# Attention and mixture of experts on one core: the inputs laid out on the host as the kernel holds them

## The chip, the core and the metric

The kernel runs on one core of a Trainium2 chip. A core has five engines that work side by side and meet at semaphores: TensorE (PE, matrix products, with weight loads PEld), VectorE (DVE), ScalarE (ACT), GpSimd (POOL) and SyncE (SP), which here only issues DMAs. SBUF is the memory that all of them work in, PSUM the one into which PE writes. The metric is the device time of one execution in microseconds.

## What is computed

Eight sequences of 256 rows of 256 numbers attend to a context of 120 rows each, and the result goes through a layer of eight experts. Biases are not zero.

```python
x = x + xattn(layernorm(x), ctx, mask)      # 16 heads of 64, keys and values from ctx (120 rows)
#   q = LN(x) @ Wq + bq ; k = ctx @ Wk + bk ; v = ctx @ Wv + bv
#   softmax(where(mask, -inf, q k^T / 8)) v, then @ Wo + bo
z = layernorm(x)
#   probs = softmax(z @ Wg), the two largest of 8, their weights normalized
#   out = sum over chosen e of w_e * (silu(z @ W1[e] + b1[e]) @ W2[e] + b2[e])
#   shared = silu(z @ Ws1 + bs1) @ Ws2 + bs2
x = x + out + 0.1 * shared
```

## The kernel before

All tensors are float32. A product is made of three on PE: each operand is split into a high part (ScalarE writes it, rounded to the PE's format, as `..._hi`) and a low part (the rest, a subtraction on VectorE or GpSimd, `..._lo`), and `three` (L301 to L305) issues high by high, high by low and low by high.

The rows are worked on in four groups of two sequences, four tiles of 128 rows each. For each group the attention runs over 8 pairs of heads (`PAIRS`); the loop variable n counts the 32 pairs of all groups, g = n // 8 and p = n % 8. In an iteration PE makes the scores of pair n, turns the probabilities of pair n - 1 (`transposes`), makes queries and keys of a later pair (`qk`), and the attention product of pair n - 1 (`attend`). VectorE takes the maxima of the scores (L673), copies the turned probabilities from PSUM (pT, L684), ScalarE takes exponentials (L1106) and writes the queries (qh, L1085), GpSimd multiplies the probabilities by their reciprocal sums (pr, L488). Each engine's order is the order of the code; there is no planner.

Before a group's queries can be made, its rows and its context must stand turned and split. In iteration p = 6 PE turns the next group's rows (`turn_rows`, L1275, into two PSUM banks) and its context (`turn_context`, L1285, four turns into bank_m). ScalarE writes the high parts xT_hi (L1070) and cT_hi (L1074), VectorE the low parts xT_lo (L648) and cT_lo (L653), in `x_turned` and then `c_turned`. ctxb holds the context as it lies in memory, 120 rows on 120 partitions.

For the first group all this stands at the start. Statistics of the rows (VectorE, L613 and L623) go to GpSimd's rsqrt (rstd, L460), VectorE normalizes (xrows, L630), PE turns. While nothing is there for PE it turns the identity (`warm`, L1290). The biases bq, bk, bv, bs1 and b1 come by five DMAs into 96 rows (brows), are turned by PE (L1433) and copied by ScalarE to bias_t (L1131), where a bias stands as a column. VectorE scales the query bias in bias_t (L734) before ScalarE may write qh. Weights come in nine pieces (`PIECES`, `load_piece`) of raw values; `piece_hi` on ScalarE (L1065) and `piece_lo` on VectorE (L636, pieces 0, 1, 4, 5) or GpSimd (L481, the others) split them:

```python
for name, h, part in (("k", 0, 2), ("q", 0, 2), ("v", 0, 1), ("v", 1, 1), ("q", 1, 2), ("k", 1, 2), ("q", 1, 1), ("k", 1, 1)):
```

A piece of part 2 is a quarter of the columns (two pairs), of part 1 a half. `next_group` on SyncE loads mask, rows and context of a later group when the tiles are free. In the attention stage GpSimd also splits the experts' second weights in pieces of 512 columns (praw, L495 and L497), which SyncE loads and stores back. After attention and the shared layer come the experts: their first weights (`load_w1`, `load_w1n`) are 1024 KB each.

## Time and profile before

| | us |
|---|---|
| median of three runs | 623.38 |
| lowest, highest | 623.11, 623.4 |
| the profiled execution | 623.21 |
| its span, first to last instruction | 621.5 |
| PE busy in it | 603.9 |
| DVE, ACT, POOL busy | 363.1, 371.6, 311.6 |

The profile is of one execution. An engine's busy time is the sum of its instructions; PE is the one that is nearly always busy. A row of the timeline shows when an instruction (or several like it in a row, as x4) starts and how long it lasts; in brackets behind it stands how long its engine had been idle and which engine's work released it. An instruction's recorded start can lie before it gets what it needs inside the engine, so a long duration of a small instruction is a wait as well.

### The profile page before, as it was taken

Reading aid. Unit: us, or ns where it says so; the run is one execution under the profiler, and the core shown is the slowest. Engines: PE = TensorE matmul, PEld = TensorE weight load, DVE = VectorE, ACT = ScalarE, POOL = GpSimd, SP = SyncE. Lnnn points to the kernel's source line nnn. Section 1 sums busy time; section 2 is a strip of 40 time slices with the busy share of each in tenths; the row PEclk is TensorE's granted clock in tenths of the full one; section 3 lists DMA queues with packets and bytes.
Section 4 is the critical chain, followed back from the end, with each engine's and each line's share of the span. In section 5 each row is a group of like instructions: output and inputs, shape, how many; then the busy total and the mean of one; then the engine's idle time right before and its main releaser. Section 6 shows DMA issues by size and latency. Waiting matters only on the chain.

```text
span 621.5 us, 13278 instructions
## 1 busy us (share of the span) xinstructions
PE 603.9 (97%) x4711; PEld 536.1 (86%) x4711; DVE 363.1 (58%) x740; ACT 371.6 (60%) x1036; POOL 311.6 (50%) x307
## 2 busy tenths in 40 slices
PE   7999999999999999999999999999999999999996
PEld 5876797779776887678988999999999999999996
DVE  5576617772577437675798444756564646564632
ACT  4778608771578428756354465948484848484742
POOL 4977527874479629745170531126443553443343
PEclk9999999999999999999999999999999999999999
DMA  9401452256234553300224449996979897989341
GB/s 291 142 2 52 137 168 90 104 164 194 92 131 138 154 187 118 100 22 0 90 86 170 139 136 279 308 377 195 327 222 332 221 360 206 335 214 324 84 138 18
DMA packets 57582, 106.35 MB, mean 171 GB/s; under 512 B 8173, under 2 KB 30734, under 8 KB 55598
## 3 DMA queue, kind: packets, MB, share of 16 engines
q1 hardware_dynamic: 42094, 63.44, 31.6%
q10 hardware_dynamic: 7840, 32.30, 14.1%
q0 software_dynamic: 7584, 9.76, 7.8%
q8 instruction: 39, 0.64, 0.4%
q14 instruction: 25, 0.20, 0.1%
HBM read 80.24 MB, written 26.16 MB: 171 GB/s over the span
## 4 chain that ended last, share of the span: by engine, by line
PE 73%; ACT 9%; DVE 8%; POOL 4%; issue 4%; DMA 1%; POOLq 0%; ACTq 0%; DVEq 0%
ACT pr L1106 7%; PE bank_s L303 4%; PE bank_t L305 4%; PE bank_t L304 4%; PE bank_t L303 4%; PE bank_s L304 4%; PE bank_s L305 4%; PE bank_s L1600 4%; PE bank_m L303 4%; PE bank_q L303 4%; PE bank_q L305 4%; PE bank_m L304 4%; PE bank_q L304 4%; PE bank_m L305 4%; PE bank_k L304 3%
## 5 line engine op out<-in xcount | busy, mean ns | idle before, releaser
L597 POOL DMA_INDIRECT out_dram<-yw,xs x39 | 65.2, 1671 | 124.2 <-DMA out_dram<-yw,xs 74.9
L1106 ACT ACTIVATE pr<-bank_s,nmax 128x120 f32<-128x120 f32 x256 | 88.2, 371 | 42.6 <-DVE nmax L673 42.3
L1007 DVE TENSOR_TENSOR hh_lo<-hbT,hh_hi 128x512 fp32r<-128x512 f32 x78 | 53.9, 692 | 68.6 <-ACT hh_hi L1236 65.8
L488 POOL TENSOR_TENSOR pr<-pr,rsum 128x480 f32<-128x480 f32 x64 | 62.7, 987 | 61.1 <-DVE rsum L677 60.7
L1233 ACT ACTIVATE hbT<-bank_s,b_col 128x256 f32<-128x256 f32 (+1 forms) x120 | 42.5, 420 | 68.2 <-PE bank_s L305 26.4
L575 POOL DMA_INDIRECT xs<-rows_d,sorted_i x39 | 44.5, 1141 | 61.9 <-issue 29.7
L1106 ACT ACTIVATION_READ_ACCUMULATOR pr<-bank_s,nmax 128x1 f32 x256 | 55.5, 217 | 0.0
L1236 ACT ACTIVATE hh_hi<-hbT 128x512 fp32r<-128x512 f32 x78 | 49.3, 632 | 2.5
L1085 ACT ACTIVATE qh<-bank_q,bias_t 128x512 f32<-128x512 f32 x32 | 22.6, 706 | 44.1 <-PE bank_q L305 41.5
L673 DVE TENSOR_REDUCE nmax<-bank_s 128x4 f32<-128x480 f32 x64 | 38.9, 650 | 6.4 <-PE bank_s L1359 5.8
L497 POOL TENSOR_TENSOR zg_lo<-praw,zg_hi 128x512 fp32r<-128x512 f32 x32 | 41.1, 1283 | 2.6
L1359 PEld LDWEIGHTS bank_s<-kh,qh 64*128 64x128 f32 x512 | 31.1, 187 | 13.0 <-issue 8.4
L1194 ACT ACTIVATE xg<-bank_s,bias_t 128x512 f32<-128x512 f32 x32 | 22.0, 688 | 32.9 <-PE bank_s L305 30.5
L684 DVE COPY pT<-bank_t 120x512 f32<-120x512 f32 x64 | 41.0, 682 | 1.0 <-PE bank_t L1371 1.0
L1359 PE MATMUL bank_s<-kh,qh 64*128 64x120 f32 x512 | 37.0, 284 | 1.8 <-ACT qh L1085 1.8
L1387 PE MATMUL bank_o<-pT,vals 120*64 120x256 f32 x256 | 34.7, 392 | 3.4 <-DVE pT L684 3.1
L1371 PE MATMUL bank_t<-ident,pr 128*120 128x128 f32 x256 | 35.9, 280 | 1.5 <-POOL pr L488 1.3
L689 DVE SCALAR_TENSOR_TENSOR aT_lo<-bank_o,bias_t,aT_hi 128x512 fp32r<-128x512 f32 x32 | 23.9, 747 | 15.9 <-ACT aT_hi L1112 15.9
L1371 PEld LDWEIGHTS bank_t<-ident,pr 128*120 128x120 f32 x256 | 27.1, 138 | 6.5 <-POOL pr L488 3.3
L1387 PEld LDWEIGHTS bank_o<-pT,vals 120*64 120x64 f32 x256 | 15.5, 136 | 14.8 <-DVE pT L684 7.0
L303 PE MATMUL bank_q<-xT_hi,wq_hi 128*128 128x512 f32 x64 | 27.6, 432 | 0.1
L495 POOL CAST zg_hi<-praw 128x512 fp32r<-128x512 f32 x32 | 19.6, 611 | 16.2 <-DMA praw<-in_L_ffn_W 16.1
(368 smaller groups left out, 2126.8 us busy)
## 6 DMA issues: line engine op xcount, KB each, us to landing
praw<-in_L_ffn_W SPq DMA_DIRECT2D x32, 256.0 KB, 2.8
w2s<-zg_hi SPq DMA_DIRECT2D x32, 256.0 KB, 3.5
w2s<-zg_lo SPq DMA_DIRECT2D x32, 256.0 KB, 3.6
aT_hi<-w2s SPq DMA_DIRECT2D x32, 256.0 KB
aT_lo<-w2s SPq DMA_DIRECT2D x32, 256.0 KB
w2n_hi<-w2s ACTq DMA_DIRECT2D x6, 1024.0 KB
w2n_lo<-w2s ACTq DMA_DIRECT2D x6, 1024.0 KB
wq_raw<-in_L_ffn_W ACTq DMA_DIRECT2D x5, 1024.0 KB
```

What stands on the lines that cost most here:

```text
L303: nc.tensor.matmul(o, st(0), mo(0), start=first, stop=False)
L304: nc.tensor.matmul(o, st(0), mo(1), start=False, stop=False)
L305: return nc.tensor.matmul(o, st(1), mo(0), start=False, stop=last)
L488: nc.gpsimd.tensor_tensor(pt, pt, rsum[:, n % 2, h, :].rearrange("p (t a) -> p t a", a=1).broadcast_to([P, GT, SK]), ALU.mult).then_inc(s[ ...
L575: nc.gpsimd.indirect_dma_start(out=xs[:, q % XU, :], out_offset=None, in_=rows_d, in_offset=bass.IndirectOffsetOnAxis(ap=sorted_i[:, ROWS[ ...
L597: nc.gpsimd.indirect_dma_start(out=out_f, out_offset=bass.IndirectOffsetOnAxis(ap=xs[:, q % XU, C:C + 1].bitcast(U32), axis=0), in_=yw[:, ...
L1007: nc.vector.tensor_tensor(hh_lo[:, n % 2, u, :], hbT[:, i % 4, :], hh_hi[:, n % 2, u, :].bitcast(F32), ALU.subtract).then_inc(s["hh_lo_s"], 1)
L1106: last = nc.scalar.activation(pr[:, n % 2, h, t, :], bank_s[h][:, t * SK:(t + 1) * SK], ACT.Exp, bias=nmax[st], accum_out=ssum[st])
L1236: nc.scalar.activation(hh_hi[:, n % 2, u, :], hbT[:, i % 4, :], ACT.Copy).then_inc(s["hh_hi_s"], 1)
L1359: last = nc.tensor.matmul(bank_s[h][:, t * SK:(t + 1) * SK], qh[r, n % 2, t * P:(t + 1) * P], kh[r, n % 2, b * SK:(b + 1) * SK], start=Fal ...
L1371: last = nc.tensor.transpose(bank_t[h][0:SK, t * P:(t + 1) * P], pr[:, n % 2, h, t, :], ident[:, :])
L1387: last = nc.tensor.matmul(bank_o[h * D:(h + 1) * D, b * S:(b + 1) * S], vals[:, b, c:c + D], pT[:, h, b * QT:(b + 1) * QT, :], start=True, ...
```

## The change

The host hands every input over in the order in which the kernel holds it; the bytes that are loaded stay the same. Rows and masks come by groups with the partition first, weights by pairs (Wq, Wk) or halves (Wv) of columns, the experts' weights with the partition ahead of the 128-row blocks, all biases as one array of 128 x 96, and the context already turned, 128 x 2 x 240. The arrays in SBUF keep their sizes, save that ctxb is now 128 partitions and brows is gone; wq, wk and wv stand in their tiles by pairs or halves, and PE's operands are read from there.

With that go: PE's four turns of the context per group, its turn of the biases, ScalarE's copy of them, and the wait of the scores for it. At the start PE turns the identity 26 times in one piece. cT_hi and cT_lo are made from ctxb and no longer from PSUM, and they come ahead of xT_hi and xT_lo for the later groups; for the first group VectorE makes cT_lo ahead of the normalized rows.

```diff
-        ctxb = sb("ctxb", [SK, GB, C], F32, a)
+        ctxb = sb("ctxb", [P, KC, GB * SK], F32, a)
...
-        for name, h, part in (("k", 0, 2), ("q", 0, 2), ("v", 0, 1), ("v", 1, 1), ("q", 1, 2), ("k", 1, 2), ("q", 1, 1), ("k", 1, 1)):
+        for name, first, size in (("k", 0, 2), ("q", 0, 2), ("v", 0, 1), ("v", 1, 1), ("q", 2, 2), ("k", 2, 2), ("q", 4, 4), ("k", 4, 4)):
...
-            eng.dma_start(w1_raw[w % W1_HOMES], w1[bass.ds(e, 1), :, :].rearrange("a (k p) n -> p (a k) n", p=P)).then_inc(w1_in[w % W1_HOMES], 16)
+            eng.dma_start(w1_raw[w % W1_HOMES], w1[bass.ds(e, 1), :, :, :].rearrange("a p k n -> p (a k) n")).then_inc(w1_in[w % W1_HOMES], 16)
...
-                    sp.wait_ge(s["ct"], g)
-                    sp.dma_start(ctxb[:, :, :], ctx_v[:, g * GB:(g + 1) * GB, :]).then_inc(s["ctx_in"], 16)
+                    sp.wait_ge(s["ct_lo"], g)
+                    sp.dma_start(ctxb[:, :, :], ctx_in[g]).then_inc(s["ctx_in"], 16)
...
                 def c_turned(g):
                     dve.wait_ge(s["ct_hi"], g + 1)
-                    nc.vector.tensor_tensor(cT_lo[:, :, :].rearrange("p k n -> p (k n)"), bank_m[:, 0:KC * GB * SK],
-                                            cT_hi[:, :, :].bitcast(F32).rearrange("p k n -> p (k n)"),
-                                            ALU.subtract).then_inc(s["ct_lo"], 1)
+                    nc.vector.tensor_tensor(cT_lo[:, :, :], ctxb[:, :, :], cT_hi[:, :, :].bitcast(F32), ALU.subtract).then_inc(s["ct_lo"], 1)
...
+                c_turned(0)
                 normalize(x_tile, "ln1", 0, lambda t: xrows[:, t, 0:C])
-                c_turned(0)
                 piece_lo(0)
...
                     if g + 1 < G and p == PAIRS - 2:
+                        c_turned(g + 1)
                         x_turned(g + 1)
-                        c_turned(g + 1)
...
-                row = 0
-                for v in (bq, bk, bv, bs1):
-                    r = v.rearrange("(a p) -> a p", p=P)
-                    act.dma_start(brows[row:row + r.shape[0], :], r).then_inc(s["brow_in"], 16)
-                    row += r.shape[0]
-                act.dma_start(brows[row:, :], b1.rearrange("e (f p) -> (e f) p", p=P)).then_inc(s["brow_in"], 16)
-                act.dma_start(wg_raw[:, :, :], wg.rearrange("(k p) n -> p k n", p=P)).then_inc(s["wg_in"], 16)
+                act.dma_start(bias_t[:, :], biases).then_inc(s["biased"], 16)
+                act.dma_start(wg_raw[:, :, :], wg).then_inc(s["wg_in"], 16)
...
                 def c_turned(g):
-                    act.wait_ge(s["ct"], g + 1)
-                    nc.scalar.activation(cT_hi[:, :, :], bank_m[:, 0:KC * GB * SK], ACT.Copy).then_inc(s["ct_hi"], 1)
+                    act.wait_ge(s["ctx_in"], 16 * (g + 1))
+                    if g:
+
+                        act.wait_ge(s["qk_k"], g * PAIRS)
+                        act.wait_ge(s["vp"], 4 * g)
+                    nc.scalar.activation(cT_hi[:, :, :], ctxb[:, :, :], ACT.Copy).then_inc(s["ct_hi"], 1)
...
-                act.wait_ge(s["b_t"], 1)
-                nc.scalar.activation(bias_t[:, :], bank_s[1][:, 0:NBIAS], ACT.Copy).then_inc(s["biased"], 1)
...
+                    if g >= 2 and h == 0:
+                        pe.wait_ge(s["lgc"], g - 1)
...
-                warm(16)
-                turn_context(0)
-                warm(8)
+                warm(26)
                 turn_rows(0)
-                pe.wait_ge(s["brow_in"], 80)
-                nc.tensor.transpose(bank_s[1][:, 0:NBIAS], brows[:, :], ident[0:NBIAS, 0:NBIAS]).then_inc(s["b_t"], 1)
-                warm(4)
                 key(0)
...
                     elif p == PAIRS - 2 and more:
                         turn_rows(g + 1)
-                        turn_context(g + 1)
```

VectorE at the start, before. xg are the raw rows, mv mean and variance, wk_lo and wq_lo the low parts of the first weight pieces:

```order
L623 BN_AGGR mv<-stats 128x2 x4
L630 TENSOR_SCALAR xrows<-xg,mv,rstd 128x256 x4
L653 TENSOR_TENSOR cT_lo<-bank_m,cT_hi 128x480
L636 TENSOR_TENSOR wk_lo<-wk_raw,wk_hi 128x2x256
L636 TENSOR_TENSOR wq_lo<-wq_raw,wq_hi 128x2x256
L648 TENSOR_TENSOR xT_lo<-bank_q,xT_hi 128x512
L648 TENSOR_TENSOR xT_lo<-bank_o,xT_hi 128x512
L642 TENSOR_SCALAR maskb<-masku 128x480
L734 TENSOR_SCALAR bias_t<-bias_t 128x8
```

The same place after:

```order
L617 BN_AGGR mv<-stats 128x2 x4
L647 TENSOR_TENSOR cT_lo<-ctxb,cT_hi 128x480
L624 TENSOR_SCALAR xrows<-xg,mv,rstd 128x256 x4
L630 TENSOR_TENSOR wk_lo<-wk_raw,wk_hi 128x512
L630 TENSOR_TENSOR wq_lo<-wq_raw,wq_hi 128x512
L642 TENSOR_TENSOR xT_lo<-bank_q,xT_hi 128x512
L642 TENSOR_TENSOR xT_lo<-bank_o,xT_hi 128x512
L636 TENSOR_SCALAR maskb<-masku 128x480
L726 TENSOR_SCALAR bias_t<-bias_t 128x8
```

cT_lo moved from behind the normalization to ahead of it.

ScalarE at the start, before:

```order
L1074 ACTIVATE cT_hi<-bank_m 128x480
L1065 ACTIVATE wk_hi<-wk_raw 128x2x256
L1065 ACTIVATE wq_hi<-wq_raw 128x2x256
L1070 ACTIVATE xT_hi<-bank_q 128x512
L1070 ACTIVATE xT_hi<-bank_o 128x512
L1131 ACTIVATE bias_t<-bank_s 128x96
L1065 ACTIVATE wv_hi<-wv_raw 128x2x512
L1085 ACTIVATE qh<-bank_q,bias_t 128x512
```

and after:

```order
L1065 ACTIVATE cT_hi<-ctxb 128x480
L1052 ACTIVATE wk_hi<-wk_raw 128x512
L1052 ACTIVATE wq_hi<-wq_raw 128x512
L1057 ACTIVATE xT_hi<-bank_q 128x512
L1057 ACTIVATE xT_hi<-bank_o 128x512
L1052 ACTIVATE wv_hi<-wv_raw 128x1024
L1076 ACTIVATE qh<-bank_q,bias_t 128x512
```

The copy of the biases between xT_hi and wv_hi is gone.

VectorE in front of the second group (iteration p = 6 and on), before:

```order
L677 RECIPROCAL rsum<-ssum 128x4 x2
L648 TENSOR_TENSOR xT_lo<-bank_q,xT_hi 128x512
L648 TENSOR_TENSOR xT_lo<-bank_k,xT_hi 128x512
L653 TENSOR_TENSOR cT_lo<-bank_m,cT_hi 128x480
L689 SCALAR_TENSOR_TENSOR aT_lo<-bank_o,bias_t,aT_hi 128x512
L673 TENSOR_REDUCE nmax<-bank_s 128x4 x2
```

and after:

```order
L669 RECIPROCAL rsum<-ssum 128x4 x2
L647 TENSOR_TENSOR cT_lo<-ctxb,cT_hi 128x480
L642 TENSOR_TENSOR xT_lo<-bank_q,xT_hi 128x512
L642 TENSOR_TENSOR xT_lo<-bank_k,xT_hi 128x512
L681 SCALAR_TENSOR_TENSOR aT_lo<-bank_o,bias_t,aT_hi 128x512
L665 TENSOR_REDUCE nmax<-bank_s 128x4 x2
```

cT_lo stands first of the three splits, and its first input is ctxb in SBUF.

## Rows read from the trace of the kernel before

**Rows 1.** The page: engine table (busy us, share, instructions) and DMA packets.

```profile
PE 603.9 (97%) x4711; PEld 536.1 (86%) x4711; DVE 363.1 (58%) x740; ACT 371.6 (60%) x1036; POOL 311.6 (50%) x307
...
DMA packets 57582, 106.35 MB, mean 171 GB/s; under 512 B 8173, under 2 KB 30734, under 8 KB 55598
```

**Rows 2.** Busy time by stage: from:to, length, busy (instructions), clock share, DMA, GB/s.

```profile
0.00:15.10 15.10, 10.45 (x58) 8.75 (x58) 9.09 (x21) 5.80 (x10) 6.77 (x18) 1.00 0.91 288
30.00:80.00 50.00, 49.25 (x383) 37.30 (x382) 32.41 (x77) 36.80 (x148) 34.03 (x36) 1.00 0.20 66
400.00:450.00 50.00, 49.79 (x426) 49.62 (x425) 28.27 (x51) 30.16 (x64) 23.78 (x16) 1.00 0.92 302
```

The engines stand in the order PE, PEld, DVE, ACT, POOL.

**Rows 3.** Timeline of the start: start us, us, engine, line, operation [idle <-releaser].

```profile
5.95 1.06 PE L1285 MATMUL bank_m<-ident,ctxb 120*128 120x120 f32 x4 [0.19 <-DMA ctxb<-in_ctx]
...
6.31 1.05 POOL L460 TENSOR_TENSOR rstd<-vareps,mhalf 128x4 f32<-128x4 f32 x1
...
7.40 1.38 DVE L630 TENSOR_SCALAR xrows<-xg,mv,rstd 128x256 f32<-128x256 f32 x4 [1.45 <-POOL rstd L460]
...
8.70 0.65 DVE L653 TENSOR_TENSOR cT_lo<-bank_m,cT_hi 128x480 fp32r<-128x480 f32 x1
...
9.53 0.60 ACT L1070 ACTIVATE xT_hi<-bank_q 128x512 fp32r<-128x512 f32 x1 [0.87 <-PE bank_q L1275]
...
10.46 0.68 DVE L648 TENSOR_TENSOR xT_lo<-bank_q,xT_hi 128x512 fp32r<-128x512 f32 x1
...
10.50 0.26 ACT L1131 ACTIVATE bias_t<-bank_s 128x96 f32<-128x96 f32 x1
...
10.63 1.07 ACT L1065 ACTIVATE wv_hi<-wv_raw 128x1024 fp32r<-128x1024 f32 x1
...
11.29 0.47 PE L303 MATMUL bank_q<-xT_hi,wq_hi 128*128 128x512 f32 x1
...
11.66 0.40 DVE L642 TENSOR_SCALAR maskb<-masku 128x480 bf16<-128x480 uint8 x1
...
11.78 2.51 POOL L481 TENSOR_TENSOR wv_lo<-wv_raw,wv_hi 128x1024 fp32r<-128x1024 f32 x1 [2.28 <-ACT wv_hi L1065]
...
11.98 2.34 DVE L734 TENSOR_SCALAR bias_t<-bias_t 128x8 f32<-128x8 f32 x1
...
14.36 0.69 ACT L1085 ACTIVATE qh<-bank_q,bias_t 128x512 f32<-128x512 f32 x1 [2.66 <-DVE bias_t L734]
...
15.10 1.16 PE L1359 MATMUL bank_s<-kh,qh 64*128 64x120 f32 x16 [1.76 <-ACT qh L1085]
```

**Rows 4.** Timeline: VectorE beside GpSimd, in two places.

```profile
18.43 3.00 POOL L467 TENSOR_TENSOR xall<-xg,bo_bc 128x512 f32<-128x512 f32 x2
...
18.93 1.34 DVE L636 TENSOR_TENSOR wq_lo<-wq_raw,wq_hi 128x512 fp32r<-128x512 f32 x1
...
286.05 1.02 POOL L460 TENSOR_TENSOR rstd<-vareps,mhalf 128x4 f32<-128x4 f32 x1
...
286.23 0.69 DVE L822 TENSOR_TENSOR aT_lo<-xg,aT_hi 128x512 fp32r<-128x512 f32 x1 [0.32 <-ACT aT_hi L1199]
```

**Rows 5.** Timeline in front of the third group, where its context is turned.

```profile
126.20 0.58 PE L1285 MATMUL bank_m<-ident,ctxb 120*128 120x120 f32 x4
...
127.24 1.08 PE L1387 MATMUL bank_o<-pT,vals 120*64 120x256 f32 x8 [0.46 <-DVE pT L684]
...
128.21 1.93 POOL L488 TENSOR_TENSOR pr<-pr,rsum 128x480 f32<-128x480 f32 x2
...
128.88 0.69 DVE L648 TENSOR_TENSOR xT_lo<-bank_q,xT_hi 128x512 fp32r<-128x512 f32 x1 [0.31 <-ACT xT_hi L1070]
...
129.85 1.09 PE L1371 MATMUL bank_t<-ident,pr 128*120 128x128 f32 x8
...
130.09 0.65 DVE L653 TENSOR_TENSOR cT_lo<-bank_m,cT_hi 128x480 fp32r<-128x480 f32 x1
...
130.69 0.48 PE L303 MATMUL bank_q<-xT_hi,wq_hi 128*128 128x512 f32 x1
```

109 lines of the change are left out of this document (54 added, 55 removed).

## The prediction

> **What bounds the kernel now.** I read the page's engine table first: TensorE (PE) is busy 603.9 us of the 621.5 us span [rows 1]. So only what lies on PE, or what makes PE wait, can move the time. The table of stages then says where PE is not full: in the first 15.1 us it is busy 10.45 us, while in 30 to 80 it is busy 49.25 of 50 and in the expert stage (400 to 450) 49.79 of 50; the granted clock is 1.00 in all three, the full level of 2.4 GHz [rows 2]. So there are two places to look at: the start, and the small waits in the attention loop. In the expert stage a faster weight load has almost nothing to win, since PE hardly waits there.
>
> The start, as the timeline shows it [rows 3]. Statistics lead to rstd on GpSimd (6.31), that to the normalized rows on VectorE (7.40 to 8.78), these to PE's turn and ScalarE's xT_hi (9.53), these to xT_lo, the mask and the scaling of the query bias on VectorE. This scaling has 8 elements per partition and takes 2.34 us, from 11.98 to 14.32. GpSimd's wv_lo, which started at 11.78 and ended at 14.29, explains it: the bias comes free when wv_lo ends. Only then can ScalarE write qh (14.36), which PE waits 1.76 us for until the first scores (15.10). The last wait of the start is thus VectorE being blocked by GpSimd.
>
> **The change, part by part.**
>
> 1. Weights, rows, masks, experts: same bytes, longer runs. Of 57,582 packets 8,173 are under 512 B [rows 1]. Nothing in the start waits for a weight piece: ScalarE's splits follow one another without a wait, and in the experts PE is full [rows 2, 3]. Cost 0, gain 0; the cover is ScalarE's and PE's own work. I allow 0.3 us either way, since x itself may land a little earlier.
>
> 2. The biases come by one DMA instead of five, a turn on PE and ScalarE's copy (10.50). ScalarE starts the next instruction 0.13 us after the copy (10.63 against 10.50), so wv_hi moves from 10.63 to 10.50 and, 1.07 + 0.08 us later, wv_lo on GpSimd to 11.65 [rows 3].
>
> 3. The context comes turned. At the start VectorE's cT_lo moves ahead of the normalization. The context is there at 5.95, when PE's turn of it starts; ScalarE then needs about 0.6 us, so cT_lo can run at 6.6 to 7.3, in a gap that lasts until 7.40. Behind the normalization VectorE has up to 0.65 us less to do (cT_lo at 8.70). But the row path does not gain all of it: xT_lo needs xT_hi, which ends at 10.13, so xT_lo starts at about 10.16 instead of 10.46. That is 0.3 us. The mask goes from 11.66 to 11.36, and the bias from 11.98 to 11.68 [rows 3].
>
> Now the two meet: wv_lo would start at 11.65 and the bias scaling at 11.68. Before, GpSimd was 0.20 us ahead; now it is 0.03 us ahead, and that is within what I can read. If GpSimd is first, the bias is free when wv_lo ends: 11.65 + 2.51 = 14.16 instead of 14.29, a gain of 0.13 us; up to 0.24 if wv_lo no longer has to wait for the mask. I take 0.2. If VectorE is first, the bias is free at about 11.8, and the next to be late is the query product itself. PE starts it at 11.29 now, and would at about 10.98 (xT_lo 0.3 earlier); it would end at 12.6, qh at 13.35, and the scores would start at 13.4 instead of 15.10: a gain of 1.7 us. I take the first, because of the 0.03 us.
>
> 4. PE loses its four context turns in front of each of the three later groups (126.20 is the second). They look like a gain of up to 0.58 us each, the length of their row, but right behind them PE sits idle 0.46 us until VectorE has copied pT (127.24) [rows 5]. The same pattern stands at 58.2 and 194.1. The turns lie in front of a wait that does not depend on them, so taking them away only lengthens the wait. Gain 0, and 0.2 us in all as the bound.
>
> 5. In those three places ScalarE and VectorE now split the context before the rows, and VectorE's cT_lo reads both inputs from SBUF (ctxb and cT_hi), where it read one from PSUM. This is the part with a price. At 18.93 VectorE split a weight piece with two SBUF inputs while GpSimd added rows (18.43): it took 1.34 us [rows 4], where cT_lo with a PSUM input takes 0.65 [rows 5]. GpSimd is at work at just this place: its two multiplications of pr run from 128.21 to 130.14. ScalarE's cT_hi would be ready where xT_hi is now, so cT_lo wants to start at 128.88, inside the first multiplication. It waits until about 129.1, runs until 129.75, and holds the second multiplication up by some 0.45 us. PE needs that one for the second half of its pr transposes (129.85 and on), whose first half ends about 130.3: the multiplication now ends at 130.6 instead of 130.14, and PE loses about 0.4 us. The rows are no later than that: xT_lo starts at about 129.75 and ends at 130.45, before PE asks for it at 130.69 + 0.4. Bounds for one place: 0, if cT_lo is not blocked, and 0.9 us, if it has to wait for both multiplications (cT_lo 130.0 to 130.65, xT_lo to 131.35, against 130.69 now, and the maxima behind it later too). I take 0.4 for each of three places: 1.2 us.
>
> What the rows show there is a full block, not a sharing. The Trainium skill says so too (SBUF — State Buffer, Who interferes with whom): a VectorE tensor_tensor with both inputs in SBUF contends with GpSimd's reads. It adds that the pair of ports is held for the whole instruction. By that, rstd on GpSimd (1.05 us) would block cT_lo at the start. This trace differs: at 286.23 VectorE ran such an operation in its usual 0.69 us, wholly inside an rstd of 1.02 us [rows 4]. So I take no block there; with the page's rule the sum would be 0.6 us more.
>
> 6. Waits that the change adds: ScalarE's c_turned waits for the last keys and values of the group, PE's first value product for the logits; both are over long before, since the last keys are made an iteration earlier. SyncE waits for ct_lo instead of ct before the next context load, a few us later with tens of us of room. Cost 0.
>
> Sum: -0.2 + 0 + 1.2 = +1.0 us against the profiled execution's 623.21 us (span 621.5 and 1.7 around it), 624.2. The median of the runs is 0.17 us above that execution, so I forecast 624.3 us.
>
> **The rivals.**
>
> A, the forecast: GpSimd stays first at the start, and the context split costs at the three places: 624.3 (623.6 to 625.0).
>
> B: VectorE's bias scaling gets in before wv_lo. For it speaks that the lead shrinks from 0.20 to 0.03 us; against it, that GpSimd's request still comes first, and may even come while the mask runs, in front of the bias in the queue. -1.7 + 1.2 = -0.5: 622.9 (622.0 to 623.5).
>
> C, on the slower side: cT_lo at the start collides with GpSimd's vareps or rstd. The normalization waits for rstd and stands behind cT_lo on VectorE, and the whole row path behind it, wv_hi and wv_lo included. If the context lands 0.35 us earlier than 5.95, cT_lo reaches VectorE before rstd starts at 6.31 and delays it by up to its own 0.65 us; if rstd holds cT_lo back instead, normalization moves from 7.40 to about 7.98. Either way +0.4 to +0.6 us. This decides from about 5.6 us of landing time on, or with the rule of part 5. -0.2 + 0.5 + 1.2 = +1.5: 624.9; with the three places at their upper bound, 625.8.
>
> D: the layout does what its words say and the split costs nothing: cT_lo is not blocked at the three places, and the turns that PE loses are worth 0.2 us. -0.4 with GpSimd first at the start: 623.0; with VectorE first -1.9: 621.5.
>
> **How the numbers follow.** A 0.47, B 0.25, C 0.16, D 0.12 (a third of it with VectorE first). The range reaches from B's lower half to C's: 621.9 to 625.7. Some 0.2% (1.25 us) is what a measurement of this kernel can tell from no change. Faster than 622.1: a third of B, a third of D, and some unknown gain of longer packets: 0.17. Slower than 624.6: a third of A, most of C, and a little for unknown costs: 0.30. The rest, 0.53, is the same.
>
> **What would show it.** In the profile after: the bias scaling on VectorE either lasts over 2 us again (A) or under 0.2 us (B), and PE's first scores start at about 14.9 or 13.4. xrows starts at 7.40 (A, B) or 7.8 and later (C). At the three places cT_lo lasts 0.8 to 1.3 us instead of 0.65, GpSimd's second pr multiplication 1.4 instead of 0.97, and PE's query product starts 0.2 to 0.6 us later behind the same pT wait (D: none of it). PE's wait for pT is longer by the turns taken away. The forecast is wrong if a part of the span between 30 and 600 us becomes shorter by more than 0.3 us, since nothing there should gain, or if the experts' stage changes.

## The result, and the profile after

The changed kernel takes 625.0 us (median of 16 runs, 624.24 to 625.65); the kernel before takes 623.39 (16 runs beside them). The ratio estimated from these runs is 1.0016, with a 95% interval of 1.0008 to 1.0023; the two medians alone are further apart, 1.6 us or 0.26%, because the times gather in two groups and the middle of the changed kernel's runs lies in the upper one: seven at 624.2 to 624.4 and nine at 625.0 to 625.7, against twelve at 623.0 to 623.9 and four at 624.2 to 624.9 for the kernel before. So the change costs 0.16% to 0.26%. The forecast was 624.3, in a range of 621.9 to 625.7, with "the same" as the likeliest case. The profiled execution took 624.37 us (span 622.6) against 623.21 (span 621.5) before, which is 1.16 us more.

The page of the changed kernel, engine table and DMA packets, to be held against [rows 1]:

```profile
PE 601.1 (97%) x4692; PEld 533.0 (86%) x4692; DVE 364.5 (59%) x740; ACT 371.8 (60%) x1035; POOL 311.2 (50%) x307
...
DMA packets 44083, 106.35 MB, mean 171 GB/s; under 512 B 6610, under 2 KB 15315, under 8 KB 38771
```

The packets fell from 57,582 to 44,083 at the same bytes, and TensorE has 2.8 us less to do. Still the span grew. Busy time by stage (from:to, length, then PE, PEld, DVE, ACT, POOL; granted clock, DMA share, GB/s), to be held against [rows 2]:

```profile
0.00:15.10 15.10, 8.40 (x50) 7.04 (x50) 9.15 (x21) 5.84 (x9) 6.93 (x18) 1.00 0.88 301
...
30.00:80.00 50.00, 48.73 (x375) 36.51 (x374) 33.11 (x77) 36.98 (x148) 34.41 (x36) 1.00 0.19 65
400.00:450.00 50.00, 49.82 (x426) 49.65 (x425) 29.25 (x52) 31.48 (x66) 22.79 (x16) 1.00 0.89 295
```

TensorE's 2 us less in the start became idle time. In 30 to 80 it is busy 48.73 us instead of 49.25, and the experts' stage is as full as it was.

**Where the time went.** I followed one event through the whole attention phase: the first scores matmul of each pair (the loop has 32 pairs, eight for a group; pairs 8, 16 and 24 open the later groups). The table gives its start in the kernel before, and how much later it comes in the others. A step in a line is a place where time is lost. The runs below the first line are the experiments of the next section.

| kernel | 0 | 7 | 8 | 15 | 16 | 23 | 24 | 31 |
|---|---|---|---|---|---|---|---|---|
| before, us | 15.10 | 60.85 | 67.93 | 128.76 | 135.86 | 196.41 | 203.75 | 262.57 |
| changed | +0.08 | +0.11 | +0.52 | +0.23 | +0.89 | +0.88 | +1.37 | +1.35 |
| 1, PSUM operand | -0.31 | -0.29 | -0.28 | -0.51 | -0.25 | -0.20 | -0.19 | -0.19 |
| 2, rows first | +0.11 | +0.14 | +0.15 | -0.10 | +0.18 | +0.22 | +0.20 | +0.22 |
| 3, cT_lo on GpSimd | +0.11 | +1.71 | +1.72 | +1.49 | +1.77 | +1.82 | +1.87 | +1.89 |
| 4, bias early | -1.17 | -1.15 | -0.73 | -0.97 | -0.27 | -0.23 | +0.32 | +0.33 |
| 5, behind vareps | +0.08 | +0.10 | +0.52 | +0.27 | +0.94 | +0.98 | +1.44 | +1.47 |
| 6, three edits | -1.09 | -1.08 | -1.07 | -1.36 | -1.09 | -1.10 | -0.99 | -1.00 |
| 7, as 6, on GpSimd | +0.08 | +0.13 | +0.14 | -0.10 | +0.12 | +0.16 | +0.32 | +0.35 |
| 8, w1 as given | +0.29 | +0.34 | +0.76 | +0.53 | +1.20 | +1.24 | +1.79 | +1.82 |
| 9, TensorE kept busy | +0.33 | +0.36 | +0.78 | +0.55 | +1.21 | +1.26 | +1.68 | +1.69 |
| 10, best | -1.22 | -1.20 | -1.18 | -1.42 | -1.14 | -1.09 | -0.96 | -0.95 |
| 11, as 10, cT_lo behind | -1.33 | -1.33 | -1.32 | -1.61 | -1.35 | -1.35 | -1.26 | -1.30 |
| 12, before again | +0.10 | +0.10 | +0.11 | +0.15 | +0.15 | +0.21 | +0.16 | +0.18 |

The changed kernel stands at +0.08 after the start. It loses 0.41, 0.38 and 0.49 us at the three later groups (the second measured from pair 14, which stands at +0.51), 1.27 us between pairs 0 and 31, and about 0.2 us come back by the end: from pair 31 to the end of the span it takes 358.7 us instead of 358.9. 0.08 + 1.27 - 0.2 = 1.15, and the profiled executions are 1.16 us apart.

**The start**, timeline of the changed kernel, to be held against [rows 3]:

```profile
5.10 0.61 ACT L1065 ACTIVATE cT_hi<-ctxb 128x480 fp32r<-128x480 f32 x1 [1.61 <-DMA ctxb<-in_ctx]
...
5.92 0.62 DVE L647 TENSOR_TENSOR cT_lo<-ctxb,cT_hi 128x480 fp32r<-128x480 f32 x1
...
6.09 0.52 POOL L450 TENSOR_TENSOR vareps<-mv,epst 128x4 f32<-128x4 f32 x1 [4.06 <-DVE mv L617]
6.69 1.05 POOL L454 TENSOR_TENSOR rstd<-vareps,mhalf 128x4 f32<-128x4 f32 x1
...
7.77 1.38 DVE L624 TENSOR_SCALAR xrows<-xg,mv,rstd 128x256 f32<-128x256 f32 x4 [1.22 <-POOL rstd L454]
...
9.21 0.66 PE L1264 MATMUL bank_q<-ident,xrows 128*128 128x128 f32 x4 [2.76 <-DVE xrows L624]
...
10.53 0.69 DVE L642 TENSOR_TENSOR xT_lo<-bank_q,xT_hi 128x512 fp32r<-128x512 f32 x1 [0.18 <-ACT xT_hi L1057]
...
12.02 2.36 POOL L475 TENSOR_TENSOR wv_lo<-wv_raw,wv_hi 128x1024 fp32r<-128x1024 f32 x1 [2.14 <-ACT wv_hi L1052]
...
12.05 2.35 DVE L726 TENSOR_SCALAR bias_t<-bias_t 128x8 f32<-128x8 f32 x1
...
15.18 1.04 PE L1338 MATMUL bank_s<-kh,qh 64*128 64x120 f32 x14 [1.76 <-ACT qh L1076]
```

The context is there about 0.85 us earlier than I assumed (cT_hi starts at 5.10; TensorE's first turn of it stood at 5.95). So cT_lo runs at 5.92, just as GpSimd wants to add epsilon to four numbers. That addition takes 0.52 us and ends at 6.61, 0.07 after cT_lo; in both traces of the kernel before it takes 0.20. In all seven experiments that keep cT_lo in this place (1 to 4 and 8 to 10) it takes 0.52 again. rstd moves from 6.31 to 6.69 and the rows from 7.40 to 7.77; 0.32 us of that is the longer addition, the rest the statistics in front of it, which end 0.06 us later. What cT_lo's move frees on VectorE is used up by that: xT_lo starts at 10.53 instead of 10.46. At 12.02 GpSimd's wv_lo is in front of the bias scaling by 0.03 us, the lead that I had worked out, and the scaling takes 2.35 us again. Note also TensorE's idle time in front of the rows, 2.76 us; before it was 0.61.

The trace of the kernel before had shown the same meeting once, after the attention:

```profile
285.25 0.66 DVE L822 TENSOR_TENSOR aT_lo<-xg,aT_hi 128x512 fp32r<-128x512 f32 x1
...
285.42 0.56 POOL L456 TENSOR_TENSOR vareps<-mv,epst 128x4 f32<-128x4 f32 x1 [6.57 <-DVE mv L623]
```

The same addition of epsilon takes 0.56 us there beside a subtraction with two SBUF operands, and ends 0.07 us after it. I had read the rows right behind these [rows 4] and not these.

**In front of the second and the third group**, the same kernel. Compare the second half with [rows 5].

```profile
61.09 1.27 DVE L647 TENSOR_TENSOR cT_lo<-ctxb,cT_hi 128x480 fp32r<-128x480 f32 x1 [0.31 <-ACT cT_hi L1065]
...
64.14 1.21 DVE L665 TENSOR_REDUCE nmax<-bank_s 128x4 f32<-128x480 f32 x2
...
127.46 1.08 PE L1366 MATMUL bank_o<-pT,vals 120*64 120x256 f32 x8 [0.59 <-DVE pT L676]
...
128.79 2.35 POOL L482 TENSOR_TENSOR pr<-pr,rsum 128x480 f32<-128x480 f32 x2
...
129.11 1.19 DVE L647 TENSOR_TENSOR cT_lo<-ctxb,cT_hi 128x480 fp32r<-128x480 f32 x1 [0.31 <-ACT cT_hi L1065]
...
131.20 0.65 PE L1350 MATMUL bank_t<-ident,pr 128*120 128x128 f32 x4 [0.47 <-POOL pr L482]
131.61 0.47 PE L298 MATMUL bank_q<-xT_hi,wq_hi 128*128 128x512 f32 x1
```

In front of the third group it is as forecast: cT_lo takes 1.19 us instead of 0.65, GpSimd's two multiplications 2.35 instead of 1.93, and TensorE has a new wait of 0.47 us between the two halves of its pr transposes. The fourth group is the same (the second multiplication takes 1.41 instead of 0.99; a wait of 0.52 at 199.55). In front of the second group the price is alike, but it goes another way. There GpSimd's second multiplication starts 0.2 us ahead of cT_lo and keeps its 0.99 us; cT_lo waits for it and takes 1.27. Everything behind it on VectorE is late: the maxima start at 64.14 instead of 63.40, and through the exponentials and qh the scores of pair 8 come 0.41 us later.

### The profile page after: what moved, and what is told of

Its sections match the earlier page's. It is cut to its first block, busy times and chain, and to the rows that moved or that the text cites. A ratio compares the mean times of both kernels' runs of the same rounds, so it can differ in the third digit from the quotient of the medians.

```text
span 622.6 us, 13237 instructions
## 1 busy us (share of the span) xinstructions
PE 601.1 (97%) x4692; PEld 533.0 (86%) x4692; DVE 364.5 (59%) x740; ACT 371.8 (60%) x1035; POOL 311.2 (50%) x307
## 2 busy tenths in 40 slices
DMA packets 44083, 106.35 MB, mean 171 GB/s; under 512 B 6610, under 2 KB 15315, under 8 KB 38771
## 4 chain that ended last, share of the span: by engine, by line
PE 72%; ACT 8%; POOL 7%; DVE 6%; issue 4%; DMA 3%; POOLq 0%; ACTq 0%; DVEq 0%
ACT pr L1097 6%; PE bank_s L298 4%; PE bank_t L299 4%; PE bank_t L300 4%; PE bank_t L298 4%; PE bank_s L300 4%; PE bank_s L299 4%; PE bank_s L1573 4%; PE bank_m L298 4%; PE bank_q L298 4%; PE bank_q L299 4%; PE bank_q L300 4%; PE bank_m L299 4%; PE bank_m L300 4%; PE bank_k L299 3%
## 5 line engine op out<-in xcount | busy, mean ns | idle before, releaser
L1222 ACT ACTIVATE hbT<-bank_t,b_col 128x256 f32<-128x256 f32 x64 | 26.7, 469 | 1.3 <-PE bank_t L300 1.3
```

The costliest lines, as they stand in the source:

```text
L1222: last = nc.scalar.activation(hbT[:, i % 4, q], bank_u[u][:, q], ACT.Silu, bias=b1_col[:, n % 2, f:f + 1])
```

## The experiments

Each of them changes the changed kernel, unless it says otherwise. Times and ratios stand beside runs of the kernel before on the same chip; the ratio is estimated from all of them and differs from that of the medians by up to 0.2%.

**1. The second operand in PSUM.** At the three later groups cT_lo reads a PSUM bank instead of ctxb; that part of the result is then not the reference's.

```diff
+                    if g:
+                        nc.vector.tensor_tensor(cT_lo[0:SK, :, :].rearrange("p k n -> p (k n)"), bank_m[0:SK, 0:KC * GB * SK],
+                                                cT_hi[0:SK, :, :].bitcast(F32).rearrange("p k n -> p (k n)"), ALU.subtract).then_inc(s["ct_lo"], 1)
+                        return
```

> The changed kernel, with one input of cT_lo at the three later groups read from PSUM (bank_m, 120 partitions, whatever stands there) instead of ctxb. Order, size and waits stay as they are; cT_lo's values are not the context's, and that part of the result is left wrong. Theory 1 (VectorE with two SBUF inputs blocks and is blocked by GpSimd): cT_lo lasts 0.65 us at all three places, GpSimd's second pr multiplication 0.97, and the scores of n = 8, 16 and 24 come 1.2 us earlier in sum than in the changed kernel: span about 621.3, ratio to the kernel before 0.999 to 1.000. Theory 2 (the order alone, context ahead of rows, makes the rows late): cT_lo lasts 0.65 too, but the loss of 1.2 us stays, span 622.4 to 622.6.

Measured: 622.83 us, ratio 0.9999 (0.9983 to 1.0014). The timeline in front of the third group:

```profile
128.05 1.94 POOL L482 TENSOR_TENSOR pr<-pr,rsum 128x480 f32<-128x480 f32 x2
...
128.38 0.66 DVE L648 TENSOR_TENSOR cT_lo<-bank_m,cT_hi 120x480 fp32r<-120x480 f32 x1 [0.31 <-ACT cT_hi L1069]
...
129.34 1.35 PE L1354 MATMUL bank_t<-ident,pr 128*120 128x128 f32 x8
```

cT_lo takes 0.66 us beside the multiplication, GpSimd's pair is back at 1.94, and TensorE's eight transposes run through. The order of the work is that of the changed kernel, so the order alone costs nothing; it takes the second SBUF operand. The steps at pairs 8, 16 and 24 are +0.01, -0.01 (from pair 14 at -0.24) and +0.01 us. At pair 15 the line dips by 0.27 us (from -0.24 at pair 14 to -0.51) and is back at 16: that is what the removed turns are worth, a gain that lasts for one pair.

**2. Rows first.** The context is split behind the rows, as the kernel before did it, still with two SBUF operands.

```diff
-                        c_turned(g + 1)
                         x_turned(g + 1)
+                        c_turned(g + 1)
```

(on ScalarE and on VectorE)

> The changed kernel with ScalarE and VectorE splitting rows first and the context last at the three later groups, as before the change; cT_lo still reads two SBUF inputs. Theory 1 (blocking by GpSimd): cT_lo now meets other GpSimd work (the cast and split of a weight piece at the first place, the bias row's addition at the other two), lasts 1.0 to 1.9 us, no longer holds up the pr multiplication, but delays aT_lo and the maxima behind it by 0.3 to 1.2 us; a loss of 0 to 0.4 us at each place against the kernel before, span 621.6 to 622.6. Theory 2 (order alone): no loss left at the three places, span 621.3.

Measured: 622.76 us, ratio 0.9984 (0.9975 to 0.9993). Timeline in front of the third group:

```profile
128.50 1.93 POOL L482 TENSOR_TENSOR pr<-pr,rsum 128x480 f32<-128x480 f32 x2
128.79 0.69 DVE L642 TENSOR_TENSOR xT_lo<-bank_q,xT_hi 128x512 fp32r<-128x512 f32 x1 [0.31 <-ACT xT_hi L1057]
...
130.00 0.94 DVE L647 TENSOR_TENSOR cT_lo<-ctxb,cT_hi 128x480 fp32r<-128x480 f32 x1
...
130.38 1.70 POOL L461 TENSOR_TENSOR xall<-xall,bs_bc 128x512 f32<-128x512 f32 x1
```

cT_lo still collides: it takes 0.94 us, and GpSimd's addition beside it 1.70 instead of 1.29. (In front of the second group cT_lo keeps its 0.65 us, and GpSimd's split of a weight piece beside it takes 1.62 instead of 1.29.) But TensorE waits for neither, and the steps are +0.01, 0.00 (from pair 14 at +0.18) and -0.02 us. So the same collision costs 0.4 us or nothing, depending on whose work GpSimd is doing just then. With experiment 1: neither the order nor the two operands cost by themselves, only both together. I had expected up to 0.4 here and was too careful. (The profiled execution of this kernel took 631.19 us: TensorE stood idle for 4.28 us up to 577.25, and its clock was at 0.75 in 570 to 580. The other eleven took 622.3 to 623.3.)

**3. cT_lo on GpSimd**, at the later groups, behind its multiplications of pr.

```diff
+                def context_lo(g):
+                    pool.wait_ge(s["ct_hi"], g + 1)
+                    nc.gpsimd.tensor_tensor(cT_lo[:, :, :], ctxb[:, :, :], cT_hi[:, :, :].bitcast(F32), ALU.subtract).then_inc(s["ct_lo"], 1)
...
                     scale(n)
+                    if g + 1 < G and p == PAIRS - 2:
+                        context_lo(g + 1)
...
                     if g + 1 < G and p == PAIRS - 2:
-                        c_turned(g + 1)
                         x_turned(g + 1)
```

> The changed kernel with cT_lo of the three later groups made by GpSimd, behind its two pr multiplications, instead of VectorE. Theory 1: GpSimd needs 1.2 us for it (480 elements; 512 take 1.28), ends at about 131.4 at the second place, before PE asks for the keys (131.9), and nothing is blocked; VectorE's xT_lo, aT_lo and maxima come 0.6 us earlier than in the kernel before: each place costs 0 or gains up to 0.3 us, span 620.6 to 621.4. Theory 2 (order): the rows are split as before, so no loss either. If GpSimd becomes the late one, PE's key product waits and each place costs up to 0.5 us: span 622 and more.

Measured: 622.87 us, ratio 0.9989 (0.9980 to 0.9998). GpSimd takes 1.22 us for it, and TensorE's transposes run through:

```profile
131.96 1.22 POOL L479 TENSOR_TENSOR cT_lo<-ctxb,cT_hi 128x480 fp32r<-128x480 f32 x1
...
131.33 1.37 PE L1355 MATMUL bank_t<-ident,pr 128*120 128x128 f32 x8
```

The steps are 0.01, 0.01 (from pair 14 at +1.76) and 0.05 us: as cheap as experiment 2. The line stands at +1.71 at pair 7 because in this execution TensorE's granted clock fell behind the wait for the first scores:

```profile
15.21 1.16 PE L1343 MATMUL bank_s<-kh,qh 64*128 64x120 f32 x16 [1.77 <-ACT qh L1081]
...
16.00:18.00 2.00, 2.00 (x13) 1.56 (x10) 1.22 (x2) 2.00 (x8) 1.82 (x1) 0.74 0.68 274
18.00:20.00 2.00, 2.00 (x9) 1.84 (x8) 0.01 (x1) 2.00 (x13) 2.00 (x3) 0.50 0.01 3
```

(The lower two lines are stages; 0.74 and 0.50 are the clock.) It took 624.42 us, the other ten 622.5 to 623.2. So this fall cost 1.6 us, and it came long after TensorE's gap in front of the rows. The kernel before has the same wait of 1.76 us in front of its first scores.

**4. The bias scaled early**, ahead of the normalization.

```diff
                 c_turned(0)
+                dve.wait_ge(s["biased"], 16)
+                nc.vector.tensor_scalar(bqk[:, 0, :], bqk[:, 0, :], SCALE, None, ALU.mult).then_inc(s["bq_s"], 1)
                 normalize(x_tile, "ln1", 0, lambda t: xrows[:, t, 0:C])
...
                 add_mask(0)
-                dve.wait_ge(s["biased"], 16)
-                nc.vector.tensor_scalar(bqk[:, 0, :], bqk[:, 0, :], SCALE, None, ALU.mult).then_inc(s["bq_s"], 1)
```

> The changed kernel with the scaling of the query bias on VectorE ahead of the normalization instead of behind the mask. Theory: the bias was late only because wv_lo on GpSimd blocked its scaling for 2.3 us; now it is scaled in 0.1 to 0.2 us before 8 us, qh starts when PE's query product ends (about 13.0) and the first scores at 13.7 to 13.9 instead of 15.18: 1.3 to 1.5 us less, and PE is the bound from there on, so the whole gain stays: span 621.1 to 621.4. Rival: the mask, which comes next on VectorE, or kh, is then blocked by wv_lo in the bias's place, and less than 0.3 us is gained: span 622.3 and more.

Measured: 622.9 us, ratio 0.9999 (0.9989 to 1.0009).

```profile
6.58 0.17 DVE L721 TENSOR_SCALAR bias_t<-bias_t 128x8 f32<-128x8 f32 x1
...
13.93 1.16 PE L1338 MATMUL bank_s<-kh,qh 64*128 64x120 f32 x16 [0.42 <-ACT qh L1076]
```

The scaling takes 0.17 us instead of 2.35, and the first scores stand at 13.93 instead of 15.18. One small instruction behind the wrong neighbour was worth 1.25 us. The three steps stay (0.42, 0.43, 0.55).

**5. cT_lo behind the addition of epsilon** at the start.

```diff
+                dve.wait_ge(s["ve"], 1)
                 c_turned(0)
```

> The changed kernel with one wait more at its start: VectorE waits for GpSimd's addition of epsilon (the semaphore ve) before it takes the first group's cT_lo. In the changed kernel that 4-element addition took 0.52 us beside cT_lo (0.20 in the kernel before), rstd ended at 6.69 (6.31) and xrows began at 7.77 (7.40). Theory 1 (cT_lo of two SBUF operands holds GpSimd off, and 0.37 us of the start is lost by that alone): the addition is back at about 0.20 us; cT_lo runs beside the power rstd (1.0 us long) and ends before it, so xrows begins at about 7.4, the first scores at 14.7 to 14.9 (15.18 in the changed kernel), the time falls by 0.2 to 0.5 us, the later drifts of +0.4 at each of the three places stay. Theory 2 (a long GpSimd operation holds VectorE's two-operand instruction off until it ends, by a lock for the whole instruction): cT_lo takes 1.0 to 1.5 us, ends at 7.3 to 7.9, normalization begins 0.2 to 0.6 us later than 7.4, and nothing or little is won at the scores.

Measured: 624.28 us, ratio 1.0007 (0.9997 to 1.0017). Timeline of the start:

```profile
6.31 0.66 DVE L647 TENSOR_TENSOR cT_lo<-ctxb,cT_hi 128x480 fp32r<-128x480 f32 x1 [0.32 <-POOL vareps L450]
...
12.91 0.16 DVE L727 TENSOR_SCALAR bias_t<-bias_t 128x8 f32<-128x8 f32 x1
...
6.07 0.20 POOL L450 TENSOR_TENSOR vareps<-mv,epst 128x4 f32<-128x4 f32 x1 [4.03 <-DVE mv L617]
6.35 1.53 POOL L454 TENSOR_TENSOR rstd<-vareps,mhalf 128x4 f32<-128x4 f32 x1
...
12.98 2.37 POOL L475 TENSOR_TENSOR wv_lo<-wv_raw,wv_hi 128x1024 fp32r<-128x1024 f32 x1 [2.97 <-ACT wv_hi L1053]
```

Both theories missed. (The 6.69 and 6.31 in the text above are where rstd begins, not where it ends.) The addition is back at 0.20 us, as theory 1 said; but rstd, which now starts 0.04 us after cT_lo, takes 1.53 us instead of 1.05, and the rows begin at 7.91. VectorE's operation kept its 0.66 us, so theory 2 is wrong too. The delay has only moved from one GpSimd instruction to the next: 0.32 us on the one, 0.48 on the other. Whatever cT_lo meets on GpSimd between the statistics and rstd's end pays, and the normalization waits for it. In this execution the bias also got in before wv_lo, by 0.07 us (12.91 against 12.98), and took 0.16 us. That is my rival B, which happened here only because everything ahead of it was late: the granted clock was 0.50 in 10 to 12 us, the key product's matmuls took 0.41 instead of 0.28, and the scores came at 15.18 all the same. Experiment 1's profile shows the same pair (clock 0.50, bias in 0.16 us), and its scores came at 14.79, 0.39 us ahead of the changed kernel's; it is the fastest of that kernel's eleven runs (622.29). So with the bias scaled late a fall of the clock at this place costs nothing here: it also lets the bias in before wv_lo.

**6 and 7. Edits together.** 6: cT_lo behind vareps, bias early, rows first. 7: the same start, and cT_lo of the later groups on GpSimd.

> Three edits together: VectorE takes the first cT_lo behind GpSimd's addition of epsilon, it scales the bias before the normalization (both in the start), and at the three later groups the rows are split first and the context last. If the effects found apart add up: scores of pair 0 at 13.5 to 13.9 us (15.18 in the changed kernel, 15.10 before), no step at pairs 8, 16 and 24 (within 0.15 us each), so the experts begin 1.1 to 1.6 us earlier than in the kernel before and the time is 621.2 to 622.2 us, 0.2 to 0.35% under it: faster than both kernels. Rival: some other wait in the rows' phase holds the clock of the pairs (as the wait for pT took 0.28 us at pair 15), and what the start wins is taken up before pair 31: drift at pair 31 within 0.5 us of the kernel before, time 622.6 to 623.4.

> As the run before, but at the three later groups GpSimd takes cT_lo, behind its two multiplications of pr, and VectorE only the rows. Start as there (pair 0 at 13.5 to 13.9). At the places 0 to +0.1 us each (GpSimd's own 1.3 us lie beside TensorE's key and query work), so 621.2 to 622.3 us, the same as the run before within 0.3. If GpSimd's two-operand subtraction holds VectorE's work off as the other way round, the rows' xT_lo and maxima come later and a step of 0.3 to 0.6 us stands at each of the three places: 622.5 to 623.6.

Measured: 6 took 622.73 us, ratio 0.9969 (0.9948 to 0.9991); 7 took 622.68, ratio 0.9988 (0.9965 to 1.0012). Their runs gather in two groups: 621.4 to 621.8 (4 of 12 and 5 of 12) and 622.4 to 623.3 (8 and 6; one of 7's took 630.3). Both medians are above what I had expected, because most runs lie in the upper group. By luck one profile fell into each. The stage 10 to 15 us of 6 (columns as above):

```profile
10.00:15.00 5.00, 4.40 (x37) 3.27 (x35) 2.51 (x5) 3.76 (x6) 2.44 (x3) 1.00 1.05 382
```

and of 7, with TensorE's first turning of rows:

```profile
10.00:15.00 5.00, 4.75 (x23) 3.84 (x21) 2.56 (x5) 2.71 (x4) 2.04 (x2) 0.72 1.05 395
...
9.34 1.11 PE L1270 MATMUL bank_q<-ident,xrows 128*128 128x128 f32 x4 [2.34 <-DVE xrows L630]
```

The two starts are the same program. With the clock at 1.00 (6) the first scores stand at 14.01, in 7 with the clock down to 0.50 of full speed (1.2 of 2.4 GHz) for some 3.4 us (worked out from the granted clock of 2 us stages: 0.84, 0.50, 0.81) at 15.18. That fall costs 1.17 us, about the distance between the groups (1.2 to 1.3 us between their means). In front of it TensorE had been idle for 2.34 us. The kernel before has 0.61 us of idle time there:

```profile
8.84 0.66 PE L1275 MATMUL bank_q<-ident,xrows 128*128 128x128 f32 x4 [0.61 <-DVE xrows L630]
```

The changed kernel and its variants have 1.7 to 2.8 us. Before, the context's turns waited for the context, and eight throwaway transposes stood behind them, until 8.2 us; now 26 throwaway transposes run in one go and end between 6.4 and 7.7. So the gap could be a hidden price of the change, and run 9 was made for it. Against it stands that the kernel before, with its gap of 0.61 us, has an upper group too: 4 of the 16 runs beside the changed kernel, 6 of 33, 13 of 35 and 6 of 17 beside the experiments lie at 624.1 or more.

**8. w1 as given.** The experts' first weight in the reference's layout again, all else as changed.

```diff
-            eng.dma_start(w1_raw[w % W1_HOMES], w1[bass.ds(e, 1), :, :, :].rearrange("a p k n -> p (a k) n")).then_inc(w1_in[w % W1_HOMES], 16)
+            eng.dma_start(w1_raw[w % W1_HOMES], w1[bass.ds(e, 1), :, :].rearrange("a (k p) n -> p (a k) n", p=P)).then_inc(w1_in[w % W1_HOMES], 16)
...
-        "w1": by_experts(ffn["W1"]), "w2": by_experts(ffn["W2"]), "b2": ffn["b2"],
+        "w1": ffn["W1"], "w2": by_experts(ffn["W2"]), "b2": ffn["b2"],
```

> The changed kernel with one layout undone: the experts' first weight lies in DRAM as the reference gives it, so its loads (in the experts' stage) read rows of 4 KB instead of one longer row for each partition; all else as in the changed kernel. It asks whether the 0.25 us (0.3 to 0.8 in other runs) that TensorE gives back to the kernel before between pair 31 and the end come from that layout. If they do: the drift against the kernel before at the last expert equals the one at the first (+1.35), and the time is 0.2 to 0.6 us above the changed kernel's, 625.2 to 625.6. If not, the drift falls by 0.25 to 0.8 us here as well, and the time is the changed kernel's within 0.2 us.

Measured: 624.57 us, ratio 1.0014 (1.0004 to 1.0024). From the scores of pair 31 to the end of the span it takes 358.5 us; the changed kernel takes 358.7 and the kernel before 358.9. The return in the experts' stage is there without the layout, so the layout of w1 isn't its cause. (The median is neither the 625.2 to 625.6 of the one expectation nor within 0.2 us of the changed kernel's 625.0: nine of the ten runs lie at 624.2 to 624.7, and only one above.)

**9. TensorE kept busy in front of the rows.**

```diff
-                warm(26)
+                warm(32)
+                pe.wait_ge(s["dv_rs"], 1)
+                warm(6)
                 turn_rows(0)
```

> The changed kernel with TensorE kept busy in the gap that the removed transposes left ahead of the first turning of rows: 32 throwaway transposes instead of 26, then a wait for rstd, then 6 more. In the kernel before TensorE was idle 0.61 us there, in the changed kernel and its variants 1.7 to 2.8 us, and three of their eight profiles show a granted clock of 0.50 in 10 to 12 us behind that gap (the bank_k matmuls 0.41 instead of 0.28 us, the first scores 0.8 to 1.2 us later than such starts without it). Theory 1 (the longer idle gap is what lets the clock fall in some executions, and makes the two groups of times 0.9 us apart, 624.2 to 624.4 and 625.0 to 625.7): the times gather in the lower group, median 624.2 to 624.5 us, and the profile shows 1.00 in 8 to 14 us. Theory 2 (the dips have nothing to do with the gap; the kernel before, with its 0.61 us, has two groups as well): both groups stay, median between 624.3 and 625.3.

Measured: 624.22 us, ratio 1.0013 (1.0003 to 1.0024). Nine of twelve runs took 623.9 to 624.4, three 625.7 to 625.8; of the changed kernel seven of sixteen lay at 624.2 to 624.4 and nine at 625.0 to 625.7. The idle time in front of the rows is 0.16 us, and the clock 1.00 throughout the start. Fewer runs lie in an upper group, as the first theory says, but three still do, 1.5 us above the others. They have no profile. This kernel keeps the wait of 1.76 us in front of the first scores, behind which the clock fell in experiment 3 at a cost of 1.6 us; that is a rival for these three, and for the upper group of the kernel before, which no run tests by itself.

**10 and 11. The best version.** 10: the transposes of experiment 9, bias early, cT_lo ahead of the normalization without a wait, rows first. 11: the same with the first cT_lo behind the normalization.

> Four edits together: the extra throwaway transposes of the run before, the bias scaled ahead of the normalization, cT_lo ahead of it without a wait (as in the changed kernel), rows split before the context at the three later groups. Without a fall of the clock the best times of the like kernel without the extra transposes were 621.4 to 621.8 us, its other ones 622.5 to 623.2. Theory 1 of the run before: nearly all times at 621.3 to 621.9, median under 622, 0.25 to 0.35% under the kernel before. Theory 2: two groups again, median 621.5 to 622.9. First scores at 13.9 to 14.0 us, no step over 0.15 us at pairs 8, 16 and 24.

> As the run before, but with the first cT_lo behind the normalization, where the kernel before had it. Theory (cT_lo ahead of the normalization costs GpSimd's rstd chain 0.37 to 0.5 us, and behind it costs VectorE's chain to xT_lo 0.65 us minus its slack, so the move is worth next to nothing either way): rstd ends at about 6.3 + 1.0 = 7.3, xrows begins at 7.4 instead of 7.77, cT_lo stands at 8.7 and xT_lo at 10.45 as before; first scores within 0.15 us of the run before (13.85 to 14.05), the same time within 0.2 us. Rival (the forecast's term: the move takes 0.2 us or more off VectorE's chain): first scores 0.2 us or more later than in the run before.

Measured: 10 took 621.55 us (621.15 to 621.57), ratio 0.9960 (0.9945 to 0.9974); 11 took 621.7 (621.40 to 621.76), ratio 0.9964 (0.9950 to 0.9978). Both beat both kernels: they are under the one before by 0.4% as the ratio goes, and by 0.3% as the medians go. All ten runs lie in one group; without the extra transposes 14 of 23 (6 and 7, less the one of 630.3) lay in the upper one. Like 6 and 7, these two have no long wait in front of the first scores (0.42 us); what sets them apart is the filled gap in front of the rows, the place of the first cT_lo, and the chip (the kernel before had 13 of 35 runs in its upper group beside 6 and 7, and 6 of 17 beside these). This supports that the idle gap lets the clock fall, with ten runs; three late runs in 9 say that it isn't the only way. The start of 10:

```profile
9.25 0.66 PE L1264 MATMUL bank_q<-ident,xrows 128*128 128x128 f32 x4 [0.43 <-DVE xrows L624]
...
13.88 1.16 PE L1338 MATMUL bank_s<-kh,qh 64*128 64x120 f32 x16 [0.42 <-ACT qh L1076]
```

and of 11:

```profile
6.33 1.05 POOL L454 TENSOR_TENSOR rstd<-vareps,mhalf 128x4 f32<-128x4 f32 x1
...
7.42 1.39 DVE L624 TENSOR_SCALAR xrows<-xg,mv,rstd 128x256 f32<-128x256 f32 x4 [1.39 <-POOL rstd L454]
8.71 0.65 DVE L647 TENSOR_TENSOR cT_lo<-ctxb,cT_hi 128x480 fp32r<-128x480 f32 x1
...
13.77 1.16 PE L1338 MATMUL bank_s<-kh,qh 64*128 64x120 f32 x16 [0.42 <-ACT qh L1076]
```

With cT_lo back behind the normalization rstd and xrows stand where they stood before (6.33, 7.42), and the first scores come 0.11 us earlier than with cT_lo ahead. So the move at the start, which I had counted as a gain of 0.2 us, gains nothing that can be told: by these two profiles it loses 0.1, by the medians it gains 0.15. The trace of 11 also shows that part 2 of the forecast was sized right: with the rows on time wv_lo starts at 11.66, where the forecast had 11.65.

**12. The kernel before once more**, unchanged, for a second trace.

> The kernel before once more, for a second trace of it. From pair 31 (262.57 us) to its end the first trace took 358.9 us; the changed kernel took 358.7, and its variants 358.1 to 358.5, with the same code for the experts. If that 0.2 to 0.8 us is a gain of the change: 358.9 again (within 0.1). If it is how executions differ: another value, anywhere from 358.1 to 359.

Measured: 623.0 us, span 621.3, with the scores of pair 31 here:

```profile
262.75 1.16 PE L1359 MATMUL bank_s<-kh,qh 64*128 64x120 f32 x16
```

From there to the end it takes 621.3 - 262.75 = 358.55 us, 0.38 less than in the first trace of the same program. The changed kernel and its variants (without 2) lie between 358.1 and 358.7. So a return of 0.2 us is within what executions of one program differ by. Whether the long rows give some 0.2 to 0.4 us on average in the experts' stage stays open: two traces of before are too few.

## Why the prediction was right, and where it was not

The forecast was 624.2 us for a profiled execution, and it took 624.37. That this is so close is in part luck: the start came out 0.28 us worse than the forecast had it, and 0.2 us that no term stands for came back at the end. The steps one by one:

1. **Layouts, 0 within 0.3.** Held, as far as the traces tell: the experts' stage differs by no more than two executions of one program. But I had listed an earlier landing only for x. It was the context that landed 0.85 us earlier, and that decided step 3.
2. **Bias by one DMA.** The term was right (11.66 in experiment 11), but in the changed kernel it did not bring wv_lo forward. ScalarE's wv_hi hangs on xT_hi, which came 0.37 us later with the rows, so wv_lo started at 12.02 and not at 11.65. The race came out as computed, GpSimd first by 0.03 us, at a later time.
3. **cT_lo at the start, -0.2.** This step failed. It assumed that cT_lo meets nothing on GpSimd. It met vareps, which was my rival C: I had put its threshold at a landing before about 5.6 us, and the context landed at 5.1. The rows came 0.37 us later, 0.32 of it by this meeting, which used up the gain, and the start ended at +0.08 instead of -0.2. The row at 285.42 of the kernel before could have told me the price. Rival C as a time (624.9) counted +0.5 against the same -0.2; the block was smaller than that, and the median of 625.0 is not owed to it.
4. **TensorE's turns, 0.** Held. Experiment 1 shows it most clearly: 0.27 us gained at pair 15 and lost at 16. In front of the second group TensorE's wait for pT grew from 0.54 to 0.95 us; in front of the fourth from 0.19 to 0.59; in front of the third from 0.46 to 0.59, and the rest is the passing gain at pair 15 (+0.51 to +0.23 in the changed kernel).
5. **cT_lo with two SBUF operands, 1.2.** Held: 1.27 us, and experiment 1 shows the cause. The mechanism was as described in two of the three places; in the first the delay ran over VectorE's maxima instead. The remedy was cheaper than I thought: the old order alone hides it.
6. **Waits, 0.** Held; none shows.

What the forecast lacked is the median. It lies 0.63 us above the profiled execution, while I had carried over the 0.17 us of the kernel before. The runs of the changed kernel fall into two groups, and more than half lie in the upper one. For the kernels that scale the bias early, experiments 6, 7, 10 and 11 point to the clock after TensorE's idle gap; I took the new order of TensorE's transposes at the start for free because TensorE wasn't on the path there, and gave it no term. What sets the changed kernel's own upper group stays open. Its one profile is of the lower group and has the clock at 1.00, and in experiments 1 and 5, which scale the bias late as it does, the fall in that place made the first scores no later (14.79 and 15.18 against 15.18). A fall behind the wait for the first scores would cost 1.6 us, going by experiment 3, which is more than the 0.9 us between its groups. Experiment 9 had fewer runs in the upper group (3 of 12 against 9 of 16), so the gap may still have a part in it.

On sharing between the engines the forecast weighed a rule of the Trainium skill (SBUF — State Buffer, Who interferes with whom; that the port pair is held for the whole instruction stands, for two SBUF inputs too, in its section SBUF: two separate sides) against the row in which VectorE ran beside rstd at its usual speed [rows 4]. The traces show both sides: where GpSimd's rstd came first, VectorE was not held (0.69 us at 286.23 in the kernel before, and 0.69 again at 287.70 in experiment 5); where VectorE came first, GpSimd was held until about its end (vareps in the changed kernel, rstd at 1.53 us in experiment 5). For longer GpSimd instructions the traces agree with the rule: wv_lo of 2.36 us held the bias scaling until 14.40, 0.02 us behind its own end, and the second multiplication of 0.99 us held cT_lo in front of the second group. So the lock for a whole instruction is in these traces, except where the GpSimd instruction is rstd.

## What to carry to other kernels

When an operand moves from PSUM to SBUF, look at what GpSimd does beside that instruction and who waits for it; if the order can be chosen, put the instruction beside GpSimd work that nobody waits for (0.4 us or nothing here). Look for tiny instructions that sit behind a long one of the other engine: 8 elements per partition cost 2.35 us, and scaling them 5 us earlier won as much as the whole change lost (1.25 against 1.16 us in the profiles). And when work is removed from TensorE ahead of a wait, its idle gap there grows; filling it cost nothing here, and in the kernels with the early bias the upper group of times (1.2 us) didn't show in ten runs.
